# A decoder layer in float32 on one core: the last pair of attention heads taken batch by batch, and the work behind it reordered

## What is computed

```python
x = rmsnorm(hidden)                                  # on a LayerNorm of the layer's x
q, k, v = x @ q_w, x @ kv_w, x @ kv_w                # 16 heads of 128 channels
attn = softmax(causal(q @ k.T * scale)) @ v
hid = hidden + attn @ o_w
x2 = rmsnorm(hid, ln2_w)
probs = softmax(x2 @ gate_w.T); top 4 of 16 experts, weights normalised
routed = sum over the 4 of weight * (silu(x2 @ w1_g) * (x2 @ w1_u)) @ w2
shared = (silu(x2 @ sh_g) * (x2 @ sh_u)) @ sh_down
out = hid + routed + shared
```

## Time and profile before

| | us |
|---|---|
| three timed runs | 628.13, 629.13, 629.26 |
| the profiled execution, its own time | 630.75 |
| the profile's span of it | 628.9 |
| PE busy | 596.8 (95%) |
| DVE busy | 441.2 (70%) |
| ACT busy | 356.2 (57%) |
| POOL busy | 315.9 (50%) |
| mean granted clock of PE | 0.989 of 2.4 GHz |

### The profile page before, as it was taken

One profiled execution on the slowest core, in us unless ns is written; L12 is line 12 of the kernel. 1 busy time (PEld: TensorE's weight loads), 2 busy tenths in 40 slices (PEclk: granted clock), 3 DMA queues, 4 the chain that ended last, 5 costly groups with the idle time before them and its releaser, 6 DMA issues.

```text
span 628.9 us, 13464 instructions
## 1 busy us (share of the span) xinstructions
PE 596.8 (95%) x4049; PEld 524.5 (83%) x4049; DVE 441.2 (70%) x1152; ACT 356.2 (57%) x1124; POOL 315.9 (50%) x400
## 2 busy tenths in 40 slices
PE   7788988999998999999999999999799999999997
PEld 4676766799877999999999999998678889999964
DVE  4695878888857777777777777777587776444424
ACT  2567887743367666566666657565554365554420
POOL 7888887301264444333344243344302778777750
PEclk9899999999999999999999999999898999999999
DMA  5998860040000200102020202023373442333428
GB/s 163 230 135 239 157 68 3 1 157 1 1 1 0 66 4 23 44 0 67 0 67 0 67 0 67 0 61 120 69 186 123 142 157 93 103 102 103 108 95 316
DMA packets 28401, 52.49 MB, mean 83 GB/s; under 512 B 4267, under 2 KB 16171, under 8 KB 28267
## 3 DMA queue, kind: packets, MB, share of 16 engines
q1 hardware_dynamic: 22787, 38.92, 23.7%
q0 software_dynamic: 4512, 12.33, 6.5%
q10 hardware_dynamic: 1056, 0.66, 0.6%
HBM read 39.31 MB, written 12.58 MB: 83 GB/s over the span
## 4 chain that ended last, share of the span: by engine, by line
PE 75%; DVE 7%; POOL 5%; DMA 5%; ACT 3%; issue 3%; SPq 1%; ACTq 0%; POOLq 0%; DVEq 0%
PE bank L235 48%; PE bank L1723 6%; PE bank L1143 3%; PE bank L1228 2%; PE bank L506 2%; PE bank L1135 2%; DMA hx<-yb 2%; PE bank L1650 2%; POOL p L627 2%; PE bank L1713 1%; PE bank L1694 1%; DMA Gf<-in 1%; PE bank L522 1%; DMA x<-in 1%; PE bank L489 1%
## 5 line engine op out<-in xcount | busy, mean ns | idle before, releaser
L280 POOL TENSOR_TENSOR p_sb<-p_sb,prec 128x256 f32<-128x256 f32 (+1 forms) x128 | 62.2, 507 | 161.0 <-DVE prec L274 161.0
L617 ACT ACTIVATE p<-bank,nmax 128x256 f32<-128x256 f32 (+1 forms) x128 | 52.5, 425 | 20.0 <-DVE nmax L609 19.4
L627 POOL TENSOR_TENSOR p<-p,rec 128x512 f32<-128x512 f32 x48 | 50.1, 1052 | 16.4 <-DVE rec L622 16.1
L1513 POOL DMA_INDIRECT yb<-acc,dst x47 | 48.5, 1032 | 15.7 <-issue 13.7
L235 PE MATMUL bank<-hTh,w3h 128*128 128x512 f32 x128 | 52.8, 413 | 0.0
L1942 DVE COPY hx<-bank 88x256 f32<-88x256 f32 x47 | 19.7, 420 | 46.5 <-PE bank L1713 46.4
L235 PE MATMUL bank<-hTh,w3l 128*128 128x512 f32 x128 | 50.5, 394 | 0.0
L235 PE MATMUL bank<-hTl,w3h 128*128 128x512 f32 x128 | 50.0, 391 | 0.0
L235 PE MATMUL bank<-G,xTh 128*128 x188 | 49.7, 346 | 0.0
L1723 PE MATMUL bank<-wd,hx 88*128 x188 | 48.3, 380 | 0.0
L267 ACT ACTIVATE p_sb<-bank,nmax 128x256 f32<-128x256 f32 x64 | 30.4, 475 | 29.2 <-DVE nmax L260 29.2
(11 more groups left out here) (267 smaller groups left out, 2057.4 us busy)
## 6 DMA issues: line engine op xcount, KB each, us to landing
Gf<-in SPq DMA_DIRECT2D x16, 352.0 KB, 5.3
qk<-staged SPq DMA_DIRECT2D x36, 128.0 KB, 6.1
staged<-qk SPq DMA_DIRECT2D x8, 512.0 KB, 8.6
w<-in SPq DMA_DIRECT2D x16, 256.0 KB, 3.4
wd<-in SPq DMA_DIRECT2D x1, 2816.0 KB
wv<-in SPq DMA_DIRECT2D x9, 256.0 KB, 3.7
wo<-in SPq DMA_DIRECT2D x9, 256.0 KB, 2.7
qk<-staged SPq DMA_DIRECT2D x18, 64.0 KB, 4.5
```

What stands on the lines that cost most here:

```text
L280: pool.tensor_tensor(p, p, r.to_broadcast(p.shape), ALU.mult).then_inc(u.pn, 1)
L617: act.activation(job.probs(n % 2)[:, k, :], job.scores()[:, k, :], ACT.Exp, bias=nmax1[:, n % 2, i:i + 1], accum_out=sums1[:, n % 2, i:i + ...
L627: pool.tensor_tensor(p, p, rec1[:, n % 2, job.stats].unsqueeze(2).to_broadcast(p.shape), ALU.mult)\
L1513: pool.indirect_dma_start(yb[:, :], bass.IndirectOffsetOnAxis(ap=dst[:, s:s + 1], axis=0), ysb[:, s % OUTS, :], None)\
```

## The change

**The last pair.** It gets functions of its own (`pe_last3`, `act_last3`, `dve_last3`, `pool_last3`); pairs 0 to 6 keep their order. Its units are taken as (0,0), (0,1), (1,0), (1,1), (0,2), (0,3), (1,2), (1,3) (head, batch): both heads of batches 0 and 1 first. O_PS[0] collects head 0, O_PS[1] head 1. The copies of the values come in slots 2 and 4 and twice behind the loop (`act_out_last`, `dve_out_last`). The side products: slot 0 has a q bank, a k bank and the first output bank of pair 6; slot 1 the second; slot 2 the third and a q bank; slot 3 a k bank; slot 4 the fourth; slots 5 and 6 the pair's own banks 0 and 1; banks 2 and 3 stand behind the last values. The copies `act_vb` and `dve_vb` of the second head's v fall away in the last pair. ACT squares tile 0 before the turned block of unit 7, tiles 1 and 2 behind it, the rest behind the last copy. ACT's split of the output weights moves from slot 6 to slot 4 and expert 0's high half from behind the pair to slot 5; the shared weights' high halves stay in slots 2, 3 and 4 but come behind the exponentials.

**Behind it.** The first half of tokens is normalised (DVE: before the output banks 2 and 3 are added), turned and given 8 zero products (before: 7 and 6 of them), then its logits are made; the second half is turned; then the gate half of the shared step 0, the logits of the second half, the up half of step 0, step 1. `dve_shared` of step 1 comes before `dve_places`. Of the lists, k = 0 follows `pe_down` of step 0, k = 1 to 3 stand between the gate and up halves of step 3, and steps 4 and 5 follow. The transfers on SP keep their list; its wait before the experts of group 1 is for the last pair's fourth q or k bank, now in slot 3.

The diff, without the conditions for the last pair that fall out of the shared slot functions, and without the arithmetic of a few short helpers (`pe_values3` is the body of `pe_pv3`):

```diff
-HEAD_WARM = (7, 6)
+HEAD_WARM = 8
...
-        n4 = Norm("n4", bank[4:8], ("stat", "var", "h", "tr", "hT", "hh", "hl"))
+        n4 = Norm("n4", bank[0:2] + bank[6:8], ("stat", "var", "h", "tr", "hT", "hh", "hl"))
...
-        def rms_scalar(act, s, src, g, made, count):
-            for t in range(GT * g, GT * g + GT):
+        def rms_scalar(act, s, src, tiles, made, count):
+            for t in tiles:
...
+        LAST = PAIRS - 1
+        N_LAST = 8 * LAST
+        F_LAST = BEFORE + PER_PAIR * LAST
+        UNITS = ((0, 0), (0, 1), (1, 0), (1, 1), (0, 2), (0, 3), (1, 2), (1, 3))
+        FILL_LAST = {0: ((0, Q_, 0), (1, K_, 0)), 2: ((2, Q_, 1),), 3: ((3, K_, 1),)}
+        FILL_PS = (0, 1, 1, 0)
+        FREED = {0: -1, 2: 0, 4: 1, 6: 2}
+        def pe_values_last(pe, u):
+            a, b = UNITS[u]
+            if u == 0:
+                pe.wait_ge(s_fe3, 2 * F_LAST)
+            if u in FREED:
+                pe.wait_ge(s_ol3, 4 * LAST + FREED[u])
+            pe_values3(pe, N_LAST + u, b, O_PS[a], a)
+        def pe_bank_last(pe, i, kind, part):
+            if i == 0:
+                pe.wait_ge(s_w3l, 2 * LAST + 2)
+            elif i >= 2:
+                pe.wait_ge(s_acc, 4 * LAST - 4 + i)
+            pe_bank3(pe, F_LAST + i, F_PS[FILL_PS[i]], 1, kind, part)
+        def pe_last3(pe):
+            for u in range(8):
+                if u == 1:
+                    pe.wait_ge(s_fe3, 2 * (F_LAST + 2))
+                elif u == 5:
+                    pe.wait_ge(s_fe3, 2 * (F_LAST + 4))
+                if u < 7:
+                    pe_scores3(pe, N_LAST + u + 1, (u + 1) % 2, *UNITS[u + 1], False)
+                if u == 2:
+                    pe_wo3(pe, LAST - 1, None, range(2, 3))
+                for i, kind, part in FILL_LAST.get(u, ()):
+                    pe_bank_last(pe, i, kind, part)
+                if u < 2:
+                    pe_wo3(pe, LAST - 1, F_LAST + 2, range(u, u + 1), outputs=3)
+                elif u == 4:
+                    pe.wait_ge(s_fe3, 2 * (F_LAST + 3))
+                    pe_wo3(pe, LAST - 1, None, range(3, 4))
+                elif u == 5:
+                    pe_wo3(pe, LAST, F_LAST + 5, range(0, 1), outputs=2)
+                elif u == 6:
+                    pe_wo3(pe, LAST, None, range(1, 2), outputs=2)
+                if u == 0:
+                    pe_pv3(pe, N_LAST - 1, LAST - 1, 1, 3, 2 * LAST - 1, False)
+                else:
+                    pe_values_last(pe, u - 1)
+                pe_transpose3(pe, N_LAST + u, u % 2, False)
+            pe_values_last(pe, 7)
+        def act_out_last(act, j):
+            i, a = divmod(j, 2)
+            act.wait_ge(u3.o, N_LAST + 2 * (j + 1))
+            act.wait_ge(s_wd3, 4 * LAST - 2 + 2 * i)
+            act.activation(o3h[:, a, i * 512:(i + 1) * 512], O_PS[a][:, :], ACT.Copy).then_inc(s_oe3, 1)
+        def dve_out_last(dve, j):
+            i, a = divmod(j, 2)
+            dve.wait_ge(s_oe3, 4 * LAST + j + 1)
+            cols = slice(i * 512, (i + 1) * 512)
+            dve.tensor_tensor(o3l[:, a, cols], O_PS[a][:, :], o3h[:, a, cols].bitcast(F32), ALU.subtract)\
+               .then_inc(s_ol3, 1)
+        def act_bank_last(act, i, kind, part):
+            act_bank3(act, F_LAST + i, F_PS[FILL_PS[i]], 1, kind, part)
+        def dve_bank_last(dve, i, kind, part):
+            dve_bank3(dve, F_LAST + i, F_PS[FILL_PS[i]], 1, kind, part)
+        def act_squares(act, tiles):
+            rms_scalar(act, n4, acc, tiles, s_acc, lambda t: 4 * LAST + t // 2 + 1)
+        def act_last3(act):
+            for u in range(8):
+                act_pt3(act, N_LAST + u - 1, (u + 1) % 2, False)
+                fills = FILL_LAST.get(u, ())
+                for fill in fills[:1]:
+                    act_bank_last(act, *fill)
+                if u < 7:
+                    act_exp(act, u3, N_LAST + u + 1, (u + 1) % 2, False)
+                for fill in fills[1:]:
+                    act_bank_last(act, *fill)
+                if u == 0:
+                    act_o3(act, 2 * LAST - 1, 1, 1)
+                elif u in (2, 4):
+                    act_out_last(act, u // 2 - 1)
+                if u == 4:
+                    act_wo3(act, LAST, False)
+                if 2 <= u < 2 + SC:
+                    act_shared_high(act, u - 2)
+                if u == 5:
+                    act_expert_high(act, 0)
+            act_out_last(act, 2)
+            act_squares(act, range(0, 1))
+            act_pt3(act, N_LAST + 7, 1, False)
+            act_squares(act, range(1, 3))
+            act_out_last(act, 3)
+            act_squares(act, range(3, NT))
+        def dve_last3(dve):
+            for u in range(8):
+                dve_pt3(dve, N_LAST + u - 1, (u + 1) % 2)
+                if u < 7:
+                    dve_max(dve, u3, N_LAST + u + 1, (u + 1) % 2)
+                if u == 2:
+                    dve_wo3(dve, LAST - 1, range(2, 3))
+                fills = FILL_LAST.get(u, ())
+                for fill in fills[:1]:
+                    dve_bank_last(dve, *fill)
+                if u < 7:
+                    dve_recip(dve, u3, N_LAST + u + 1, (u + 1) % 2)
+                for fill in fills[1:]:
+                    dve_bank_last(dve, *fill)
+                if u < 2:
+                    dve_wo3(dve, LAST - 1, range(u, u + 1))
+                elif u == 4:
+                    dve_wo3(dve, LAST - 1, range(3, 4))
+                elif u in (5, 6):
+                    dve_wo3(dve, LAST, range(u - 5, u - 4))
+                if u == 0:
+                    dve_o3(dve, 2 * LAST - 1, 1, 1)
+                elif u in (2, 4):
+                    dve_out_last(dve, u // 2 - 1)
+                if u == 1:
                     dve.wait_ge(s_lb, DONE + 32)
                     dve.tensor_copy(lowb[:, :], cst[:, C_LOWB:C_LOWB + P]).then_inc(s_lb, 1)
                     dve.memset(onesb[:, :], 1.0).then_inc(s_lb, 1)
-            return slot
-        def pool_slot3(pool):
-            def slot(p, a, b, u, first, last, end):
-                if last and (a, b) == (1, 2):
-                    pool_wo3(pool, p)
-                if not end:
-                    pool_normalise(pool, u3, 8 * p + u + 1, (u + 1) % 2)
-                if u in (2, 5) and not last:
-                    pool_w3(pool, 2 * p + int(u == 5) + 2, int(u == 5))
-                if (a, b) == (0, 3) and not last:
-                    pool_wv3(pool, p + 1)
-                if (a, b) == (1, 3) and not last:
-                    pool_wo3(pool, p)
-                if last and 2 <= u < 2 + SC:
+            dve_out_last(dve, 2)
+            dve_pt3(dve, N_LAST + 7, 1)
+            dve_out_last(dve, 3)
+        def pool_last3(pool):
+            for u in range(8):
+                if u < 7:
+                    pool_normalise(pool, u3, N_LAST + u + 1, (u + 1) % 2)
+                if u == 4:
+                    pool_wo3(pool, LAST)
+                if 2 <= u < 2 + SC:
                     pool_shared_low(pool, u - 2)
...
-        LG_PS, PF_PS, LS_PS = (bank[1], bank[3]), bank[4], bank[5]
+        LG_PS, PF_PS, LS_PS = (bank[3], bank[5]), bank[4], bank[5]
...
         def pool_moe(pool):
+            rms_gpsimd(pool, n4, 0)
             pool_index(pool)
-            for g in range(2):
-                rms_gpsimd(pool, n4, g)
+            rms_gpsimd(pool, n4, 1)
             pool.wait_ge(s_xd, DONE + STORED)
...
         def act_moe(act):
-            for g in range(2):
-                act_hT4(act, g)
-            for g in range(2):
-                hT_scalar(act, n4, g, high=True)
+            act_hT4(act, 0)
+            hT_scalar(act, n4, 0, high=True)
+            act_hT4(act, 1)
+            hT_scalar(act, n4, 1, high=True)
             act.wait_ge(s_rt, 4)
...
-            if v == 1:
-                pe.wait_ge(s_rt, 4)
+            if v == 1 and halves[-1]:
+                pe.wait_ge(s_rt, 2)
...
         def pe_moe(pe):
+            pe_wo3(pe, LAST, None, range(2, 4))
+            pe.wait_ge(u3.ex, 2 * 4 * H3)
+            transposes(pe, n4, h, 0)
+            pe_zeros(pe, HEAD_WARM, bank[4])
             pe.wait_ge(s_gate, 16)
-            for g in range(2):
-                pe_zeros(pe, HEAD_WARM[g], bank[0])
-                transposes(pe, n4, h, g)
-            for g in range(2):
-                pe_logits(pe, g)
-            pe_gate_up(pe, 0)
-            pe_gate_up(pe, 1, (0,))
+            pe.wait_ge(s_pl3, 2 * 4 * H3)
+            pe_logits(pe, 0)
+            transposes(pe, n4, h, 1)
+            pe_gate_up(pe, 0, (0,))
+            pe_logits(pe, 1)
+            pe_gate_up(pe, 0, (1,))
+            pe_gate_up(pe, 1)
             pe_prefix(pe)
-            pe_gate_up(pe, 1, (1,))
+            pe_gate_up(pe, 2)
             pe_down(pe, 0)
-            pe_gate_up(pe, 2)
-            for k in range(TOPK):
+            pe_list(pe, 0)
+            pe_gate_up(pe, 3, (0,))
+            for k in range(1, TOPK):
                 pe_list(pe, k)
```

(34 more changed lines are left out.)

110 lines of the change are left out of this document (49 added, 61 removed).

## The result

The changed kernel takes 637.75 us (median of four runs, 636.19 to 640.22) against 629.13 us (628.13 to 629.26): a ratio of 1.0136, interval 1.0114 to 1.0158. It is slower, by more than the range allowed (up to 634.8 us). Its profiled execution took 637.55 us, span 635.7; that of before had 630.75 and 628.9.

A forecast was written before the change was run, and what follows sets the result against it. TensorE, busy 95% of the span, was taken as the bound. +0.8 and +0.2 made +1.0 without the clock; +1.7 of clock gave +2.7 us: 633.4 profiled, 631.8 us forecast against the median 629.13, range 627.5 to 634.8.

The forecast's parts named there:

- the first apply: Norm of the first half of tokens on VectorE: 453.2 to 454.9, ahead of the two output adds.
- the lists: Shared steps behind the pair: list of k = 0 at 476.4, lists ending 3.7 us later, no clock fall counted.
- The loop: Last pair, slots 2 to 7, VectorE and ScalarE: copies lengthen the slots, output bank 2 comes 1.1 us later.
- Values 7: Start of the last unit's values on TensorE in the last pair, put at 450.0.
- The clock in the pair: TensorE's longer pauses in the last pair let the clock fall twice, 1.1 and 0.6 us, +1.7 together.
- a fall in slot 5: Low clock after TensorE's pause from 437.9 to 440.9, slowing bank 0 and the values of unit 4; 1.1 us.
- rival 2: Clock stays up but for the end of the pair; 629.1 to 630.4 us, no change that can be told; chance 0.22.
- The norm: Behind the pair: second apply 1.8 us later, half the logits in its shade, +0.7 us at the first gate product.
- The wait: TensorE ahead of the first list, since VectorE's product of step 1 stands ahead of the places; 1.5 us.
- VectorE's chain behind the lists: Later lists bring VectorE's work about level with the down step that waits for it; +0.2 us, 0 to 0.7.
- Rival 3: Faster: early first half worth more than counted, second apply before about 457.7; 626.7 to 627.8 us, chance 0.18.
- Rival 4: The last pair's waits don't move at all, bank 2 at 451.1; no chance of its own.

The follow-up runs named there:

- after: The changed kernel in its first profiled execution, against the kernel before; ratio 1.0136.
- before_warm: The kernel before with six and seven zero products in TensorE's pauses in slots 6 and 7 of its last pair; 630.42 us, ratio 1.0000.
- after_again: The changed kernel, unaltered, timed again against the kernel before; 637.76 us against 629.88, ratio 1.0131.
- old_lists: The changed kernel with everything from the logits on in the order of the kernel before; 634.86 us, ratio 1.0074.
- warm_list: The changed kernel with 6 zero products ahead of the first list, in TensorE's wait for VectorE; ratio 1.0059.
- index_late: The changed kernel with GpSimd's three conversions of index tables moved behind the second root and second apply; ratio 1.0078.
- warm_end: The changed kernel with 6, 4 and 5 zero products ahead of the values of units 6 and 7 and output bank 2; ratio 1.0044.
- list_row: The changed kernel with list 0 moved behind the gate half of step 3, so the four lists run in a row; ratio 1.0060.
- before_warm2: before_warm with two further zero products each behind lists 1 and 2; ratio 1.0010 to the kernel before.

## Why the prediction was wrong

The direction and the mechanism in the pair were right. Two steps behind it failed: the first apply, taken at its old length, and the lists, behind which the clock's fall was put at nothing. The sum was +2.7 us and the slots came +6.2 late. By terms:

- **The loop, right.** Predicted turned blocks 427.9, 432.4, 435.8, 440.2, 443.9, 447.15; measured on before's count 428.14, 432.72, 436.11, 440.50, 444.24, 447.50. TensorE standing 437.9 to 440.9: measured 438.5 to 441.2. Values 7 at 450.0: measured 450.53. At equal clock the pair is 3.0 us longer (values 7 at 33.1 in after, 30.1 in before_warm, no fall ahead of either); the fall in before's slots hides 1.4 of that, as the prediction's comparison with the row as it stood had it. The loop was undersized by 0.5 to 0.6: 0.24 in slots 0 and 1 (I had named 0 to 0.5 and taken 0), 0.1 in slot 2, and 0.2 in slot 7; slots 3 to 6 were right to 0.05.
- **The clock in the pair, right.** I took 1.1 for a fall in slot 5 and 0.6 for one at the end. Measured: 1.3 for the first; 2.4 at the banks for the second (after_again against old_lists), of which the queue of squares covers most, as foreseen: against warm_list it is 0.7 at the gate product. One of the two falls was there in every trace of the new pair, both in two; after had only the second. That is the clock of rival 2, and the time wasn't rival 2's 629.1 to 630.4 us: what failed lies behind the pair.
- **The norm, wrong.** I wrote that the residuals and applies take what they took before, 1.7 us (453.2 to 454.9), and looked only at VectorE's and ScalarE's queues. The diff moves `pool_index` between the two roots; I passed over it. It costs 1.0 us. From the banks' end to the gate product with all logits I had 9.1 us, 0.4 less than before's 9.5; warm_list has 9.7 (8.0 + 1.7), 0.6 over my count, and index_late 8.7.
- **The lists, wrong.** The wait was foreseen (1.5, measured 1.25), and so was the place of the lists: 476.4, measured 478.29, 1.9 late as all ahead of it. But I counted the shared steps behind it at full clock and took 0 for a fall there, so that the wait was set off against a fall I had struck out of before. The fall stayed in every trace, for 3.4 us or more. From gate product to slots I had +0.3 over before: -1.4 for before's fall, +1.5 for the wait, +0.2 for VectorE's chain behind the lists. In after it was +3.6: the wait measured 1.25, the fall cost 3.0, and the chain 0.6 (from the third down step to the slots 10.86 us, against 13.01 less a step of 2.8; 0.35 of it a wait of TensorE for step 4's product); less 1.4 that is 3.4 to 3.5. Where the fall was short it was +2.2 to 2.4 (warm_end, after_again, warm_list), and list_row brought that down to 0.4.

The terms close, to a tenth. For after, from the predicted +2.7: -1.1 for the fall in slot 5 that it didn't have, +0.1 for the one at the end, +0.6 loop, +0.6 norm, +3.3 from gate product to slots (3.6, and 0.3 was counted) are 6.2. For after_again: +0.2, +0.1, +0.6, +0.6 and +1.9 give 6.1, measured 6.2. That both come to 6.2 is chance: after had the longer fall at the lists, after_again one more in the pair.

What stays open is the rest: the medians are 7.9 and 8.6 apart and the profiled executions 6.8, 1.34 of it from ahead of the change. Before's profiled execution lay 1.6 above its own median. Which falls its other executions had isn't shown by any trace. The mean granted clock of each is on record: 0.978 to 0.987 in the nine of the changed kernel, 0.984 to 0.992 in sixteen of before timed beside after_again. The clock lost doesn't give the time by itself, though: two executions of after_again at 0.978 and 0.987 took 637.75 and 637.66 us.

Rival 3 put its point at the second apply, earlier than 457.7; it came at 461.45. Rival 4 is out: everything moved.

## What to carry over

Replay a reordered loop from the rows, as here; it held to half a us. Then go through the diff once more by engine, and for each moved instruction ask both who waits behind it in its queue and what runs beside it at its new place. A pause just ahead of a run of narrow products can cost more than its length (1.25 us of waiting, and the four traces of eight with an early fall took another 1.0 us or so): put a piece of work into it that has to be done anyway. Don't count a stretch of low clock as gone until a trace shows that it didn't move, and price it by the wide products that lie in it, not by its length. And compare two traces only after seeing whether the clock fell at the same places in both.

## What the hardware showed

- The clock fell in every trace within 1.0 to 7.9 us of the start of the first list (32 products of 94 columns, 5.75 us in a row, 0.18 apart), with TensorE shown busy 1.00 when it did. Six wide products (1.3 us) ahead of them (warm_list) or two pairs among them (before_warm2) didn't prevent it.
- These products take the same time at either clock: 24 of them 4.36 us at 1.00 and 4.37 at 0.50. The eight 128x256 products of a down step took 1.89 us at 1.00 and 3.64 at 0.50.
- A fall avoided at one place can come at the next: 3.4 us of clock lost in before, in before_warm and in before_warm2, in different places.
- Identical code fell at different places in different executions (after and after_again), while their turned blocks ahead of the first fall agreed to 0.02 us.
- VectorE's two-input apply and GpSimd's conversions slowed each other, 1.67 to 2.67 us and 0.50 to 0.69.
